# The reciprocal root of a layer's variances: from a GpSimd power to ScalarE's logarithm and exponential with one Newton step on VectorE

## What is computed

```python
def _layernorm(x, axis=-1, eps=1e-05):
    m = jnp.mean(x, axis=axis, keepdims=True)
    v = jnp.var(x, axis=axis, keepdims=True)
    return (x - m) / jnp.sqrt(v + eps)
...
    x = _layernorm(x + _L0_gnn_ref(x, adj, ...))   # attention over the neighbours, 4 heads of 16
    x = _layernorm(x + _L1_gnn_ref(x, adj))        # (adj + I) x / degree
    x = _layernorm(x + _L2_gnn_ref(x, adj, ...))   # adj (x W) + bias
    x = _layernorm(x + _L3_gnn_ref(x, adj))        # 1 where adj x > 0.5
```

## Time and profile before

| | before |
|---|---|
| median of the runs | 1572.43 us |
| profiled execution | span 1570.0 us |
| PE busy | 1379.7 us (88%) |
| DVE busy | 1273.9 us (81%) |
| ACT busy | 1235.0 us (79%) |
| POOL busy | 1061.9 us (68%) |

### The profile page before, as it was taken

The page is one execution under the profiler, slowest core; times in us unless marked ns, Lnnn a source line. Parts: engine busy times, 40 slices in busy tenths (PEclk is TensorE's granted clock), DMA queues, the critical chain, the costliest instruction groups (busy, mean ns, idle before and its releaser), DMA issues.

```text
span 1570.0 us, 21762 instructions
## 1 busy us (share of the span) xinstructions
PE 1379.7 (88%) x7584; PEld 689.3 (44%) x7584; DVE 1273.9 (81%) x1518; ACT 1235.0 (79%) x1428; POOL 1061.9 (68%) x566
## 2 busy tenths in 40 slices
PE   4698799999899999999989988999899989799766
PEld 2343344454445444444444544454444444345323
DVE  1689789888898878888878888988889878878864
ACT  2598788887888878888878888888888888788631
POOL 3176866778677766787657876777767876776412
PEclk9899789999999989999979999999999999999977
DMA  7634433343433433343433434335333433200000
GB/s 107 111 42 81 47 73 67 56 54 58 88 43 77 47 65 62 58 71 38 83 62 54 57 52 95 45 64 61 51 75 62 69 38 73 58 14 16 26 11 10
DMA packets 144980, 91.16 MB, mean 58 GB/s; under 512 B 102420, under 2 KB 132570, under 8 KB 144858
## 3 DMA queue, kind: packets, MB, share of 16 engines
q1 hardware_dynamic: 129382, 70.44, 21.0%
q0 software_dynamic: 14288, 18.70, 14.8%
q10 hardware_dynamic: 1200, 0.63, 0.2%
HBM read 103.33 MB, written 21.38 MB: 79 GB/s over the span
## 4 chain that ended last, share of the span: by engine, by line
PE 50%; DVE 15%; issue 13%; ACT 9%; POOL 9%; DMA 2%; SPq 1%; ACTq 0%; DVEq 0%; POOLq 0%
PE M L607 10%; PE Z L568 10%; PE M L662 9%; PE Z L570 8%; POOL LS L501 7%; DVE RP L904 5%; ACT LS L754 5%; PE Z L581 4%; DVE LS L918 4%; PE Z L676 3%; PE Z L616 2%; ACT LS L762 2%; DMA adj_cast<-in_adj_dram 1%; PE Z L730 1%; DVE X L1000 1%
## 5 line engine op out<-in xcount | busy, mean ns | idle before, releaser
L501 POOL TENSOR_TENSOR LS<-LS,MB 125x1000 f32<-125x1000 f32 x372 | 871.1, 2359 | 360.7 <-DVE LS L918 264.8
L754 ACT ACTIVATE LS<-Z 125x1000 f32<-125x1000 f32 x576 | 576.3, 1002 | 143.5 <-PE Z L570 142.6
L762 ACT ACTIVATE LS<-LS 125x1000 f32<-125x1000 f32 x576 | 596.7, 1037 | 70.5 <-POOL LS L501 53.8
L904 DVE TENSOR_TENSOR RP<-LS,RP 125x1000 f32<-125x1000 f32 x480 | 575.4, 1199 | 88.3 <-ACT LS L754 66.3
L568 PE MATMUL Z<-AT,BI 126*125 126x500 fp8e4 x1152 | 375.9, 409 | 104.7 <-ACT LS L754 73.9
L570 PE MATMUL Z<-FS,FO 96*125 96x500 bf16 x1152 | 353.1, 388 | 0.0
L607 PE MATMUL M<-LS,V 125*18 125x500 f32 x2304 | 318.3, 626 | 5.5 <-ACT LS L762 5.5
L918 DVE TENSOR_TENSOR LS<-LS,MB 125x1000 f32<-125x1000 f32 x204 | 306.1, 1505 | 7.7 <-DMA MB<-row_maxima 2.4
L568 PEld LDWEIGHTS Z<-AT,BI 126*125 126x125 bf16 x1152 | 126.7, 142 | 418.2 <-ACT LS L754 219.2
L570 PEld LDWEIGHTS Z<-FS,FO 96*125 96x125 bf16 x1152 | 164.5, 143 | 95.0 <-issue 14.8
L662 PE MATMUL M<-AT,XP 125*128 125x500 fp8e4 x756 | 192.3, 377 | 0.0
(11 more groups left out here) (136 smaller groups left out, 885.0 us busy)
## 6 DMA issues: line engine op xcount, KB each, us to landing
MB<-row_maxima SPq DMA_DIRECT2D x48, 500.0 KB, 4.0
adj_cast<-in_adj_dram POOLq DMA_DIRECT2D x96, 183.1 KB, 4.4
FO<-PARTS SPq DMA_DIRECT2D x180, 46.9 KB, 2.1
FS<-PARTS SPq DMA_DIRECT2D x180, 46.9 KB, 2.1
XP<-in_x_dram SPq DMA_DIRECT2D x8, 336.0 KB
XA<-in_x_dram SPq DMA_DIRECT2D x8, 336.0 KB
out_dram<-X SPq DMA_DIRECT2D x7, 375.0 KB
AT<-adj_cast SPq DMA_TRANSPOSE x144, 2.8
```

Of the source, the lines that this page charges most:

```text
L501: nc.gpsimd.tensor_tensor(rows, rows, MB[:P, u % 2, :, :], ALU.subtract).then_inc(sub_pool, 1)
L754: nc.scalar.activation(LS[:P, q % RL, :, :], banks("Z", q)[:P], ACT.Prelu, alpha=SLOPE).then_inc(bent, 1)
L762: nc.scalar.activation(rows, rows, ACT.Exp, scale=0.25).then_inc(exps, 1)
L904: nc.vector.tensor_tensor(run, rows, run, ALU.max).then_inc(maxed, 1)
```

## The change

`power` is taken out of POOL's program. ACT gets `root`, at the same step (+3), after `bend` and before `high`, `take`, `take_features` and `expo`: it waits for `var_ok`, writes the logarithm of the 12 sums into a new tile `ROOT`, waits for itself, and takes the exponential with scale -0.5 in place. DVE's `scale`, still at +4, waits for `root_ok` in place of `rstd_ok` and does one Newton step for the reciprocal root in three instructions on 125 x 12 numbers, each of which waits for the one before; the last writes `M1` and so stands where the copy stood.

```diff
-        NHALF = sb("NHALF", [P, NT], f32)
+        NHALF = sb("NHALF", [P, ST], f32)
+        ROOT = sb("ROOT", [P, NT], f32)
...
-            def power(b, l):
-
-                pool.wait_ge(var_ok, 4 * b + l + 1)
-                nc.gpsimd.tensor_tensor(RSTD[:, :], RSTD[:, :], NHALF[:, :], ALU.pow).then_inc(rstd_ok, 1)
...
-                if layer_at(q, POWER):
-                    power(*layer_at(q, POWER))
...
-                nc.gpsimd.tensor_tensor(part, part, NHALF[:, 0:ST], ALU.pow).then_inc(end_rstd, 1)
+                nc.gpsimd.tensor_tensor(part, part, NHALF[:, :], ALU.pow).then_inc(end_rstd, 1)
...
+            def root(b, l):
+
+                act.wait_ge(var_ok, 4 * b + l + 1)
+                nc.scalar.activation(ROOT[:, :], RSTD[:, :], ACT.Ln).then_inc(logged, 1)
+                act.wait_ge(logged, 4 * b + l + 1)
+                nc.scalar.activation(ROOT[:, :], ROOT[:, :], ACT.Exp, scale=-0.5).then_inc(root_ok, 1)
...
                 if q < QN:
                     bend(q)
+                if layer_at(q, POWER):
+                    root(*layer_at(q, POWER))
                 at = layer_at(q, HIGH)
...
                 dve.wait_ge(m1_read, order["S", b, l])
-                dve.wait_ge(rstd_ok, 4 * b + l + 1)
-                nc.vector.tensor_copy(M1[:P, 0:NT], RSTD[:, :]).then_inc(factors_in, 1)
+                dve.wait_ge(root_ok, 4 * b + l + 1)
+                nc.vector.scalar_tensor_tensor(out=RSTD[:, :], in0=RSTD[:, :], scalar=-0.5, in1=ROOT[:, :],
+                                               op0=ALU.mult, op1=ALU.mult).then_inc(refined, 1)
+                dve.wait_ge(refined, 2 * (4 * b + l) + 1)
+                nc.vector.tensor_tensor(RSTD[:, :], RSTD[:, :], ROOT[:, :], ALU.mult).then_inc(refined, 1)
+                dve.wait_ge(refined, 2 * (4 * b + l) + 2)
+                nc.vector.scalar_tensor_tensor(out=M1[:P, 0:NT], in0=RSTD[:, :], scalar=1.5, in1=ROOT[:, :],
+                                               op0=ALU.add, op1=ALU.mult).then_inc(factors_in, 1)
                 dve.wait_ge(factors_in, 4 * b + l + 1)
```

More of the change, by code:

```diff
@@ L194, in adj_resnorm @@
         var_ok = sem("var_ok")
-        rstd_ok = sem("rstd_ok")
+        logged = sem("logged")
+        root_ok = sem("root_ok")
+        refined = sem("refined")
         factors_in = sem("factors_in")
```

## The result

The changed kernel takes 1642.3 us (median of 4, 1637.4 to 1647.9) against 1573.7 for the kernel before on the same chip: ratio 1.045, interval 1.041 to 1.050. It is slower, by about 71 us (0.045 times 1572; 64 to 78 with the interval). The forecast was 1638 us. The profiled execution has a span of 1637.8 us, 67.8 more than the 1570.0 before.

A forecast was written before the change was run, and what follows sets the result against it. The prediction took PE as the bound, held up in places by ACT's `bend`. It summed 58 us of block delays and 8 us of clock to 66, on 1570.0 profiled: 1636, forecast 1638 us as median, range 1590 to 1700.

The forecast's parts named there:

- The table: On ACT at each root: two function-table loads, one before the logarithm, one before the exponential, 2.57 us together.
- Rival (a): At ACT's roots no table is loaded, since one set serves everything; block 0.5 us, 1578 us, the same; chance 0.07.
- The block: ACT held at each of 28 roots by loads, logarithm and exponential: 3.1 us each, 87 us of ACT.
- Layer 1: 3.1 + 1.1 forecast: Root of layer 1 (mislabelled layer 3): PE loses all 3.1 us a graph, plus 1.1 us for slower clock.
- its term for the clock: PE's matmuls slower after one new long wait: 1.1 us in each of seven graphs, 8 us in all.
- Layer 2: 2.7 forecast: Root of layer 2 (mislabelled layer 1): ACT waits for the sums, then loads; `bend` and PE's fill 2.7 us late a graph.
- Layer 3: 1.5 forecast: Root of layer 3 (mislabelled layer 2): PE's fill waits for a later `bend` and loses 1.5 us a graph.
- Layer 0: 1.0 forecast: Root of layer 0: loss between 0.5 (PE's fill) and 3.1 us (DVE's `rest` waiting for ACT's copy); 1.0 taken a graph.
- DVE: nothing forecast: Three small DVE instructions at each root add 0.4 us, 11 us in all; counted at nothing.
- Rival (b): Faster: no table load, and taking the power off POOL gains its 13.9 us of the chain; 1562 us; chance 0.05.
- Rival (c): Two loads a root; all 28 blocks reach PE and each costs the clock: 1696 us; no separate chance given.
- rival (d): Two loads a root; half of the 66 us caught up where PE waits for others: 1605 us; no separate chance given.

The follow-up runs named there:

- the kernel with the block alone: Kernel before, power kept on POOL, plus a logarithm and exponential of a constant with table loads on ACT at every root, nobody waiting: 1632.8 us, ratio 1.040.

## Why the prediction was right, and which of its steps were not

**The table.** Two loads a root, 57 in all, 1.283 us each, is what the profile shows (56 at the roots and the one at the start). This was the step on which all hung, and it was argued, not read: the trace of before had one load and no logarithm. It came out as taken. Rival (a) falls. Its rule in the Trainium skill (ScalarE: Activation LUTs, Table sets: the hidden batching unit) holds for the set and not for the placement: the set exists and serves everything, as the kernel with one line more shows, but it isn't chosen here unless the program names it.

**The block.** Forecast 3.1 us. Here is the root of layer 1, the stretch of the earlier trace rows, in the changed kernel, start, length, instruction, idle before it:

```profile
697.23 1.00 ACT L750 ACTIVATE LS<-Z 125x1000 f32<-125x1000 f32 x1
...
697.89 4.56 POOL L504 TENSOR_TENSOR LS<-LS,MB 125x1000 f32<-125x1000 f32 x2 [3.58 <-DVE LS L923]
698.24 1.28 ACT L816 ACT_TABLE_LOAD   x1
...
699.54 0.21 ACT L816 ACTIVATE ROOT<-RSTD 125x12 f32<-125x12 f32 x1
...
701.06 0.21 ACT L818 ACTIVATE ROOT<-ROOT 125x12 f32<-125x12 f32 x1
701.18 0.57 ACT L764 ACTIVATE O<-M 128x500 f32<-128x500 f32 x1
701.38 1.09 DVE L1001 SCALAR_TENSOR_TENSOR RSTD<-RSTD,ROOT 125x12 f32<-125x12 f32 x1 [1.15 <-ACT ROOT L818]
...
701.80 0.81 PE L587 MATMUL M<-AT,DS 125*18 125x500 fp8e4 x12 [2.46 <-ACT O L764]
...
702.58 0.99 ACT L750 ACTIVATE LS<-Z 125x1000 f32<-125x1000 f32 x1
...
703.71 1.86 PE L612 MATMUL Z<-E,O 128*125 128x36 f32 x8 [1.10 <-ACT LS L750]
...
705.51 1.87 PE L603 MATMUL M<-LS,V 125*18 125x500 f32 x8
...
707.31 1.09 PE L564 MATMUL Z<-AT,BI 126*125 126x500 fp8e4 x2
...
708.20 1.04 PE L566 MATMUL Z<-FS,FO 96*125 96x500 bf16 x2
...
709.27 1.00 ACT L750 ACTIVATE LS<-Z 125x1000 f32<-125x1000 f32 x1 [2.23 <-PE Z L566]
```

From the first load at 698.24 to `take` (L764) at 701.18 are 2.94 us. Nothing follows a load that would be a gap: the logarithm starts 0.02 us after it. The 1380 ns for a drain that the Trainium skill names (ScalarE: Activation LUTs, What ACT_TABLE_LOAD costs) don't appear here.

**Layer 1: 3.1 + 1.1 forecast, 5.4 measured.** The mechanism was right in the main, and the size off. The next `bend` starts at 702.58, 5.35 after the one before it, where the earlier trace rows have 2.28: 3.07 late. The wait isn't where it was forecast: `turn_sums` (L612) was to wait near 3.7 us for `bend` and waits 1.10, and PE has already stood for 2.46 us at L587, which needs `take`, queued on ACT behind the block. Behind that stall PE works slowly. L612 takes 1.86 where it took 1.03, L603 takes 1.87, L564 1.09 and L566 1.04. In the kernel before, the last three and the `bend` after them were:

```profile
678.50 1.03 PE L607 MATMUL M<-LS,V 125*18 125x500 f32 x8
...
679.47 0.64 PE L568 MATMUL Z<-AT,BI 126*125 126x500 fp8e4 x2
...
679.94 0.59 PE L570 MATMUL Z<-FS,FO 96*125 96x500 bf16 x2
...
680.73 1.03 ACT L754 ACTIVATE LS<-Z 125x1000 f32<-125x1000 f32 x1
```

The four groups take 0.83 + 0.84 + 0.45 + 0.45 = 2.6 us more, where the forecast had taken 1.1 from two groups in another place. PE's granted clock is 1.00 from 697 to 703 and 0.51 from 703 to 709.9, practically the lower of its two levels; in the kernel before it was 1.00 from 674 to 683. Over all seven stretches of layer 1 the records of before have no time at the lower level, and those of the changed kernel 58 us, as have those of the kernel with the block at layer 1 alone. From `bend` at 674.10 to `bend` at 680.73 were 6.63 us, and now from 697.23 to 709.27 12.04: 5.41 more, and no stretch behind it gives it back. In the kernel with the block at layer 1 alone the seven stretches cost 5.1 to 5.8 us each. This is the step of the forecast that was mis-sized most, its term for the clock: 8 us for the whole kernel, against 7 x 2.3 = 16 at layer 1 alone.

**Layer 2: 2.7 forecast, 0.6 measured.** Two things were wrong. Here is the root of layer 2 in the first graph; it is the place of the earlier trace rows, which show the second graph:

```profile
361.50 1.00 ACT L750 ACTIVATE LS<-Z 125x1000 f32<-125x1000 f32 x1
...
362.53 1.28 ACT L816 ACT_TABLE_LOAD   x1
363.01 0.42 DVE L995 TENSOR_SCALAR RSTD<-RSTD 125x12 f32<-125x12 f32 x1
...
363.82 0.21 ACT L816 ACTIVATE ROOT<-RSTD 125x12 f32<-125x12 f32 x1
...
365.35 0.21 ACT L818 ACTIVATE ROOT<-ROOT 125x12 f32<-125x12 f32 x1
...
370.74 1.00 ACT L750 ACTIVATE LS<-Z 125x1000 f32<-125x1000 f32 x1
```

The sums are ready at 363.43. The forecast let ACT wait for them and load afterwards. The load starts at 362.53, 0.90 us before they are ready: it is a step of its own ahead of the waiting logarithm, and covers the wait. From the end of `bend` at 362.50 to the `bend` of 370.74, three steps on, are 8.24 us against 6.98: 1.26 late, not 2.7. And the forecast let nothing be caught up. Half of that is gone two steps further, and the stretch ends between -1.2 and 2.2 us in the seven graphs, 0.6 on average. ACT's waits for POOL's subtraction, 53.8 us and 23.4 now, may be what takes it up; that is argued only. The run with blocks at layers 2 and 3 bears out the small cost; how it divides between the two reasons is read from this trace only.

**Layer 3: 1.5 forecast, 0.2 on average in the traces, and not well known.** `bend` is 3.1 late here too, and as much as 4.0 a few steps on in the graph shown. Ten steps later most of it is given back, and 0.7 is left at the end of the stretch. In the kernel before, POOL stood and waited for the maxima to come through the DMA (SP's rows are the issues of DMAs):

```profile
965.86 0.47 SPq L421 DMA_DIRECT2D out_dram<-X  x1
...
966.43 3.31 SPq L382 DMA_DIRECT2D row_maxima<-LMAX  x2
...
976.53 5.58 POOL L501 TENSOR_TENSOR LS<-LS,MB 125x1000 f32<-125x1000 f32 x2 [6.19 <-DMA MB<-row_maxima]
```

and in the changed kernel:

```profile
1004.06 0.47 SPq L424 DMA_DIRECT2D out_dram<-X  x1
...
1007.19 0.78 SPq L385 DMA_DIRECT2D row_maxima<-LMAX  x2
...
1015.13 5.04 POOL L504 TENSOR_TENSOR LS<-LS,MB 125x1000 f32<-125x1000 f32 x2 [2.20 <-DMA MB<-row_maxima]
```

The wait was 6.19 us and is 2.20 in this graph. The issue of the maxima follows 0.1 us on the end of the output's before, and 2.7 us in the changed kernel, and takes 0.78 us instead of 3.31: before, the maxima stood in line behind SP's other issues, and now they come when the line is empty. POOL's subtraction starts 25.8 us after the `bend` at the start of the stretch in both. A delay of 3 us was hidden behind a queue that was busy anyway. The other traces bear this out: at this place the four kernels with the loads at layer 3 have waits of 2.1 to 2.2 us, and the seven without them 4.3 to 7.7. What it leaves in the time is best told by the run with blocks at layers 2 and 3: 6 us for both, 0.5 us a block.

**Layer 0: 1.0 forecast, 3.1 measured.** The bounds were 0.5 and 3.1, and the lower was the wrong one to go near. DVE's `rest` waits for ACT's copy behind `root`. DVE waited 11.1 us for it before and 28.2 now (L957 for L789, in the view of the waits). The kernel with the block alone has 28.7 there and 15.8 us in its stretch; the two with blocks at other layers only have 12.7 and 13.2. The lower clock has its part here too: the records show 20 us of it in the seven stretches of layer 0 before and 55 now. That this chain carries the loss is argued, not tried, and so is how much of it is the clock's.

**DVE: nothing forecast, and nothing that can be told in this kernel, by luck.** "Three at about 0.2 are 0.6 us" took its price from instructions with one SBUF operand. In the kernel before, the copy into PSUM gave the multiplication behind it such an operand as well. The hold is up to 2.17 us, 19 us in all where the loads don't cover it.

**POOL: nothing forecast, nothing that can be measured.** The run without any root gives -2 us with an interval of -8 to +3. Rival (b) needed this relief and falls with it. Rival (c), all blocks arrive and each costs the clock, is near what happens at layer 1; at layers 2 and 3 less arrives than the half of rival (d).

**In short.** The forecast was right in the loads, in the size of the block and in its reaching PE. It was wrong in the clock (too small), in the place of PE's wait at layer 1, in letting nothing be caught up at layers 2 and 3, and in the price of the Newton step; that the sum came out at 66 is luck.

## What to carry to other kernels

A function that ACT's loaded table lacks costs two loads of 1.28 us each time it is used between others, and the cure is to name at the start a set that holds them all; here one line was worth 44 us. (For this kernel that only undoes a part of the loss: the power that was replaced cost it nothing that can be told.) What a block of 3 us on an engine costs depends on the place: 5.1 us at one root, about 0.5 at two others. So a forecast should replay each place up to the point where something else waits anyway, and price PE's slower matmuls behind a new stall by every group in that stretch. A DVE instruction with two operands in SBUF isn't priced by its size alone while POOL is at work: 0.17 us became 2.17 here. Look for it in the spread between the median and the maximum of such groups.

## What the runs showed of the hardware that I had not expected

- A table load is executed ahead of the wait of the instruction that needs it, and so can cover it: it started at 362.53, the sums came at 363.43.
- A DVE instruction on 125x12 with both operands in SBUF took 2.16 or 2.17 us instead of 0.17 at seven roots, ending with POOL's subtraction each time; with one operand in PSUM none of 84 took over 0.2. One that began at the change from one of POOL's instructions to the next wasn't held.
- PE's four groups behind a stall of 2.46 us took 2.6 us more than at full clock, nearly as much as the stall.
